# Two parts instead of three in the in-place loading of patches, with the picks, an exponent and a store moved, in a patch-wise expert convolution on one core

## The reference

```python
n = (x - mean_hw(x)) / sqrt(var_hw(x) + 1e-5)          # per image and channel
p = pad(n, 8 rows and columns right and below; 1 all round)
patched = windows of 10 x 10 at steps of 8              # 25 patches per image, 32 channels each
logits = mean(patched) @ Wg + bg                        # 8 experts
routing = one_hot(argmax(logits)) * softmax(logits)
outs[e] = relu(conv3x3(patched, Wexp[e]) + bexp[e])     # 'SAME' on each patch
y = sum over e of routing[e] * outs[e], inner 8 x 8 of each patch, put back in place
out = x + y[:, :, :32, :32]
```

## Time and profile before

| what | us |
|---|---|
| median of 3 runs (lowest, highest) | 192.06 (191.08, 193.27) |
| the profiled execution's own time | 194.34 |
| its span, first to last instruction | 192.5 |
| PE busy on matmuls | 107.7 |
| DVE busy | 120.5 |
| ACT busy | 90.2 |
| POOL busy | 75.1 |
| mean granted TensorE clock | 0.815 of full |

### The profile page before, as it was taken

How to read it: one execution, slowest core, us unless ns; L and a number is a source line. 1 busy time by engine, 2 the same in 40 slices (tenths; PEclk the granted TensorE clock), 3 DMA queues, 4 the chain that set the end, 5 groups by cost and what they waited for, 6 DMA issues and landing times.

```text
span 192.5 us, 11462 instructions
## 1 busy us (share of the span) xinstructions
PE 107.7 (56%) x4894; PEld 103.0 (54%) x4894; DVE 120.5 (63%) x271; ACT 90.2 (47%) x252; POOL 75.1 (39%) x236
## 2 busy tenths in 40 slices
PE   0003180495396703974199708990599356949940
PEld 0003080495396603964199608990599255939940
DVE  4699961292199338980899168942999166284274
ACT  2594136856572257346572549352745622650000
POOL 0760348074503463045613435343605563556000
PEclk9999998559969975699756985596559969995896
DMA  5974996366779898999989998998899698898602
GB/s 180 505 301 189 235 368 240 134 234 145 244 185 416 200 340 238 334 322 248 315 263 386 175 386 223 413 199 336 227 372 298 252 222 324 235 279 261 249 0 109
DMA packets 40545, 50.93 MB, mean 265 GB/s; under 512 B 31024, under 2 KB 33200, under 8 KB 39472
## 3 DMA queue, kind: packets, MB, share of 16 engines
q1 hardware_dynamic: 36880, 37.73, 63.7%
q10 hardware_dynamic: 3648, 13.02, 17.6%
HBM read 17.32 MB, written 14.43 MB: 165 GB/s over the span
## 4 chain that ended last, share of the span: by engine, by line
DMA 33%; PE 25%; SPq 20%; DVE 9%; issue 5%; ACTq 4%; ACT 2%; DVEq 0%
PE conv_bank L523 21%; DMA XG<-windows 19%; SPq L175 15%; DMA XG<-XG 12%; SPq L145 5%; PE pick_bank L511 3%; DMA XT<-x 3%; ACT WS L442 2%; ACTq L125 2%; ACTq L135 2%; DVE STATS L266 1%; DVE BLK L338 1%; DVE WP L361 1%; DVE ROWSUM L282 1%; DVE BLK L342 1%
## 5 line engine op out<-in xcount | busy, mean ns | idle before, releaser
L523 PE MATMUL conv_bank<-XG,WS 128*32 128x64 f32 x4800 | 94.7, 252 | 47.3 <-DMA XG<-XG 43.2
L523 PEld LDWEIGHTS conv_bank<-XG,WS 128*32 128x32 f32 x4800 | 90.2, 131 | 49.4 <-DMA XG<-XG 44.7
L223 POOL COPY WS<-WP 128x192 f32 x200 | 61.5, 355 | 94.9 <-issue 63.4
L442 ACT COPY WS<-WP 128x192 f32 x200 | 54.7, 348 | 66.3 <-issue 38.7
L331 DVE STREAM_TRANSPOSE YT<-conv_bank 128x320 f32<-128x320 f32 x40 | 19.6, 502 | 16.5 <-PE conv_bank L523 16.5
L266 DVE BATCH_NORM_STATS2 STATS<-XT 128x6 f32<-128x512 f32 x16 | 10.2, 680 | 26.4 <-DMA XT<-x 26.4
L338 DVE STREAM_TRANSPOSE BLK<-YT 128x1024 f32<-128x1024 f32 x8 | 17.9, 2242 | 1.1
L505 PE MATMUL logit_bank<-GATE,CONST 128*100 128x8 f32 x40 | 5.8, 253 | 20.7 <-DVE GATE L296 20.7
L434 ACT COPY WIND<-XN 128x2500 f32<-128x2500 f32 x7 | 16.6, 2375 | 0.2
L505 PEld LDWEIGHTS logit_bank<-GATE,CONST 128*100 128x100 f32 x40 | 4.9, 188 | 21.7 <-issue 15.6
L511 PE MATMUL pick_bank<-PROB,CONST 100*128 100x1 f32 x36 | 8.4, 338 | 9.3 <-DVE PROB L314 9.3
(11 more groups left out here) (37 smaller groups left out, 49.1 us busy)
## 6 DMA issues: line engine op xcount, KB each, us to landing
XG<-XG SPq DMA_DIRECT2D x30, 490.0 KB, 3.9
windows<-WIND ACTq DMA_DIRECT2D x8, 1250.0 KB
XG<-windows SPq DMA_DIRECT2D x60, 125.0 KB, 3.4
XT<-x SPq DMA_DIRECT2D x8, 512.0 KB, 6.1
XG<-XG SPq DMA_DIRECT2D x16, 240.0 KB
out<-XT SPq DMA_DIRECT2D x7, 512.0 KB, 6.0
XG<-windows SPq DMA_DIRECT2D x32, 62.5 KB, 2.7
XG<-ones ACTq DMA_DIRECT2D x1, 1250.0 KB, 11.2
```

The costliest lines, as they stand in the source:

```text
L223: last = nc.gpsimd.tensor_copy(WS[:, at % RING, ACT_PAIRS + i, :], WP[:, bass.ds(index[i], PAIR)])
L442: last = nc.scalar.copy(WS[:, at % RING, i, :], WP[:, bass.ds(index[i], PAIR)])
L523: last = nc.tensor.matmul(o, WS[:, lot, n % LOT * 2 + b // 2, column:column + C], taps, start=kx == 0, stop=kx == TAPS - 1)
```

## The change

`PART` is (0, 2, 5): lots 0 and 1, and lots 2, 3 and 4. SP's queue has one later part instead of two, so four readings and two shifts fewer in each group, each of the remaining ones as large as both were together, and its store now stands behind the readings of part 1. PE computes the picks after lot 1. Ahead of the loop, ACT takes the exponent of group 1 before the root of group 2, both right behind the copies of lot 1, and DVE takes routing and probability of group 1 before the deviation of group 2. In all later turns DVE's and ACT's order is as before.

```diff
-PART = (0, 2, 4, LOTS)
+PART = (0, 2, LOTS)
...
             read_upper(0, 1)
-            read_upper(0, 2)
             shift(sp, 0, 1)
-            shift(sp, 0, 2)
...
-                if g > 0:
-                    store(g - 1)
                 if g + 1 < GROUPS:
                     shift(sp, g + 1, 0)
                     read_upper(g + 1, 1)
-                    read_upper(g + 1, 2)
+                if g > 0:
+                    store(g - 1)
+                if g + 1 < GROUPS:
                     shift(sp, g + 1, 1)
-                    shift(sp, g + 1, 2)
...
             statistics(2)
+            routing(1)
+            probability(1)
+            deviation(2)
 
             for g in range(GROUPS):
-                if g + 1 < GROUPS:
+                if 0 < g and g + 1 < GROUPS:
                     routing(g + 1)
-                if g + 2 < GROUPS:
+                if 0 < g and g + 2 < GROUPS:
                     deviation(g + 2)
-                if g + 1 < GROUPS:
+                if 0 < g and g + 1 < GROUPS:
                     probability(g + 1)
-                else:
+                if g + 1 == GROUPS:
...
             write_windows(1)
-            for lot in range(1, LOTS - 1):
-                copies(0, lot)
+            copies(0, 1)
+            exponent(1)
             root(2)
+            copies(0, 2)
+            copies(0, 3)
             for g in range(GROUPS):
                 copies(g, LOTS - 1)
-                if g + 1 < GROUPS:
+                if 0 < g and g + 1 < GROUPS:
                     exponent(g + 1)
...
                     last.then_inc(conv_done, 1)
-                    if lot == 0:
+                    if lot == 1:
                         pe.wait_ge(pick_ready, turn)
                         pe.wait_ge(own_ready, turn)
                         picks()
```

More of the change, by code:

```diff
@@ L201, in _ @@
                     load_x(g + 3)
+                if g + 1 < GROUPS:
+                    shift(sp, g + 1, 0)
+                    read_upper(g + 1, 1)
                 if g > 0:
@@ L204, in _ @@
                 if g + 1 < GROUPS:
-                    shift(sp, g + 1, 0)
-                    read_upper(g + 1, 1)
-                    read_upper(g + 1, 2)
                     shift(sp, g + 1, 1)
-                    shift(sp, g + 1, 2)
             for q in range(2):
```

## The result

The changed kernel takes 208.92 us (median of 4 executions, 208.19 to 209.99), the kernel before 192.67 (4 executions, 191.08 to 194.26). The ratio is 1.088, 95% interval 1.077 to 1.099: the change costs 8 to 10%. The profiled execution's span is 207.8 us.

A forecast was written before the change was run, and what follows sets the result against it. Part 1's circle was to bound the kernel: T(0) 48 + 5 × 22.8 + 2 × 19.9 + end 7.9 = 209.7 us span, forecast 209 after allowing for the profiled execution; own range 201 to 217, 8 in 10 from 188 to 216.

The forecast's parts named there:

- the circle through part 1: Last lot, next group's part 1 reading, shifted copies, windows' write, lots 2 to 4: 22.8 us with write, 19.9 without.
- Start: Group 0: the 7.28 us wait goes, lot 2 waits for its shift; T(0), its last lot's end on PE, 48 us.
- Reading: Part 1's four DMAs of 187.5 KB from the window buffer into XG, 5.3 us (4.7 to 5.8).
- Shift with the write: Part 1's two shifted copies, 5.9 us, plus 2.9 for meeting the windows' write in the DMA engines.
- Three lots: Lots 2 to 4 on PE after the long wait, partly at 1.2 GHz: 8.6 us (7.1 to 9.9).
- Sum: Last lot to last lot: five steps of 22.8 us, two of 19.9; with start and end a span of 209.7.
- Part 0: Lots 0 and 1 and their reading and shift: off the path, landing before the last lot; lots about 3.7 us.
- "worth nothing" for the store: Store moved behind part 1's reading: part 0's shift up to 0.8 us sooner, worth nothing while part 0 is off the path.
- Picks: Picks, 1.2 us, leave part 0's circle for PE's new gap: worth nothing, 1.2 if the gap were gone.
- Lots at 2.4 GHz: Rival, chance 0.13: part 1's lots keep full clock, last lot to last lot 19.5 to 20 us with write, 189 us.
- Write out of the way: Rival, chance 0.13: the windows' write avoids part 1's shift, all seven steps 19.9 us, 195 us.
- Part 0 as the bound: Rival, chance 0.10: part 0's circle stays the bound, start, picks and store gain 12, last group loses 3: 183 us.

The follow-up runs named there:

- the run with the late write: Changed kernel with each windows' write made to wait until the shift of part 1 under way has landed: 197.1 us, ratio 1.020 against the kernel before.
- the filling: Changed kernel with eight unread 128x512 matmuls behind each group's picks, to keep TensorE busy in its wait: 204.1 us (197.2 to 205.7).
- the three-part kernel: Kernel before with the first exponent ahead of the root and picks behind lot 1, three parts and store place kept: 186.3 us, ratio 0.964.

## Why the prediction was right, step by step

The forecast was 209 and the kernel takes 208.9, with its own reason: the circle through part 1. The agreement to 0.1 us is luck, since terms missed in both directions. It is luck in the last step too: the predicted span was 209.7 and the measured one is 207.8, but the forecast took the median to be 2.3 us below the profiled execution, as it was before, and it is 0.7 below (208.9 and 209.6).

- **Start.** T(0) 48, measured 49.1. The next late thing was the shift of part 1, as said, but it took 8.1 us (30.54 to 38.62) instead of 5.9: lot 2 at 38.7 instead of 36.9. PE's waits named "issue" came again (1.33 and 1.56 us there, 1.65 in lot 1).
- **Reading.** 5.3, measured 5.4, 6.4, 6.0, 5.9 and 5.7 in the five steps with a windows' write: 0.6 too small. The store that was put behind it is a likely part of the reason: with it at its old place the second to the fifth step had 5.6 to 5.7 on average instead of 6.0. In the last two steps, with a store and no write, the readings took 5.6 and 5.3.
- **Shift with the write.** 5.9 + 2.9 = 8.8, measured 9.3, 9.7, 9.7, 9.7 and 9.2, mean 9.5; without the write 6.6 and 5.5 against 5.9. The meeting costs 3.5, above the 0 to 2.9 that the prediction allowed, and taking it away gave 3.4 (the run with the late write). The 2.9 was the difference of two stages, and 1250 KB at the 371 GB/s of the earlier trace rows would be 3.5 us (an estimate). "DMA: Bandwidth & Descriptors", "Queues, rings and completion order", in the Trainium skill says that each engine takes turns between its queues by whole packets; the trace agrees in so far as SP's shift is held up by 3.5 us, about the time of ACT's whole write; the turns themselves no run here shows.
- **Three lots.** 8.6, measured 6.4, 6.9, 7.4, 7.7 and 6.6, mean 7.0. This is the term that was mis-sized: I took the mean length of the slow stretches of group 2 and on, 7.2 us, of which the earlier trace rows show two; here three lots in 7.0 us are 3.5 us at half clock and 3.5 at full, and over the seven steps, of 6.4 to 7.7 us, the slow stretch so worked out is 2.3 to 4.9 us. The direction was right: 1.8 us above 5.25.
- **Sum.** 22.8 per step with a write, measured 22.6 on average; 19.9 without, measured 18.7. End 7.9, measured 207.8 − 199.9 = 7.9, from the turning of the last lot as in the earlier trace rows.
- **Part 0.** Off the path, as said; lots 0 and 1 took 3.56 (5.16 the first time), predicted 3.7. Its shift lands in time in all steps.
- **The step that failed:** "worth nothing" for the store. It was weighed only for part 0, and not as a piece between reading and shift of part 1, on the very circle that I had just named. By the two traces with the store at its old place it costs about 1 us there in each step that also has a windows' write, which the too long lots made up for. The rule would have been to ask of the moved DMA what stands behind it in the queue.
- **Picks.** Nothing was forecast for the two-part kernel, and no run moves them alone there; all three other edits together are 208.9 against 207.9. "1.2 if the gap were gone" was for the other circle; with three parts they give 3.6 us in all.
- **Rivals.** Lots at 2.4 GHz: the filling shows steps of 19.9 and 21.9 with fast lots, so the clock alone would not have brought 189; the fastest execution with the filling took 197.2. Write out of the way: 197.1, where I gave 195. Part 0 as the bound: not in two parts; its claim that start and picks are gains, of 12 us, is true of the three-part kernel in kind, at 8 us (186.3 against 194.3).

Most of the profile's signs came: order of the chain, the wait ahead of lot 2 (6.2 to 11.6 us, forecast 7 to 10), logits 21.3 to 23.5 us apart and then 19.7 and 17.7 (forecast 22 to 24, then 20), DMA share near 0.8, and none of the signs of being wrong. One came in part only: the 360 matmuls were to take over 7 us at a clock near 0.5; they took 6.5 to 7.8, at a granted clock of 0.50 in their first 2 us and of 0.65 to 0.80 over the whole. The rule of the Trainium skill's page "TensorE: Matmul & The Clock Gate", section "HAM oscillation", that the prediction names, a throttled start of every burst that waits for a DMA, holds behind all seven long waits of this kernel.

What stays open: how the 7.5 us that the store costs with three parts divide over all steps between its data, the longer meeting with the write and the clock; how much later the windows' write must be issued to spare the shift (issued 0.3 to 1.6 us behind the shift's first issue it cost some 3 us, and once, at 2.2 us, nothing); and why one wait of 3.85 us left the clock high while one of 3.39 did not, nor one of 2.70 in the run with the late write, behind which three lots took 7.8 us.

## What to carry to other kernels

Where a buffer is overwritten in place, write down for each part the circle of its own (last reader, read, dependent copy, compute) with all that it meets in the queues; merging parts saves issues but lengthens that part's circle by the merged data and by the compute that had run beside it. A change of several edits can hide a good one: here exponent and picks make 0.964 of the time, the store and the parts lose it again. A DMA that nobody waits for still has to be placed by what stands behind it in its queue.

## What was unexpected of the hardware

- Handing over four readings of 125 KB took SP 5.7 to 6.0 us when shifts of 1480 KB and the windows' write were under way, 1.4 us each, and 4.2 us behind such shifts alone, against 0.6 to 0.7 each for larger ones (187.5 KB, 2.62 us for four) in an emptier queue.
- A store of 512 KB, moved in the queue from ahead of one shift to ahead of the next ones, cost 7.5 us in the three-part kernel.
- Waits of 8 to 12 us before a burst left TensorE slow for no longer than shorter ones: three lots took 6.4 to 7.7 us behind them, and 7.5 to 7.9 behind waits of 2.7 to 5.6 us in the run with the late write.
